# Edge keys broadcast by DMA in place of 51 transpositions on TensorE

## The reference

```python
mask = jnp.full((N, N), -jnp.inf, dtype=dtype)
mask = mask.at[src, dst].set(w[edge_type - 1])      # 6528 edges, N = 384
```

## Time and profile before

| | us |
|---|---|
| median of 3 runs | 727.94 |
| lowest and highest | 725.6, 729.39 |
| profiled execution | 726.86 |
| its span | 725.1 |
| TensorE matmuls busy | 702.6 |
| VectorE busy | 476.5 |
| ScalarE busy | 402.0 |
| Pool busy | 229.2 |

### The profile page before, as it was taken

The page is one execution under the profiler, slowest core; times in us unless marked ns, Lnnn a source line. Parts: engine busy times, 40 slices in busy tenths (PEclk is TensorE's granted clock), DMA queues, the critical chain, the costliest instruction groups (busy, mean ns, idle before and its releaser), DMA issues.

```text
span 725.1 us, 11736 instructions
## 1 busy us (share of the span) xinstructions
PE 702.6 (97%) x4490; PEld 669.4 (92%) x4490; DVE 476.5 (66%) x957; ACT 402.0 (55%) x692; POOL 229.2 (32%) x203
## 2 busy tenths in 40 slices
PE   3999999999999999999999999999999998999987
PEld 3989999998999999999999999998899998889886
DVE  6758774874777477766666565656766466787543
ACT  5455556464565565768686775422523457677340
POOL 4634332232332332227022274470004511422120
PEclk9999999999999999999999999999999999999998
DMA  5421635413313223231313152234135749896242
GB/s 212 160 107 59 231 138 211 176 60 120 109 67 117 73 102 117 90 118 58 117 59 117 59 209 73 109 121 138 41 136 193 272 164 378 307 413 220 117 145 88
DMA packets 21766, 105.15 MB, mean 145 GB/s; under 512 B 5696, under 2 KB 6080, under 8 KB 12912
## 3 DMA queue, kind: packets, MB, share of 16 engines
q1 hardware_dynamic: 12880, 80.84, 30.4%
q0 software_dynamic: 8544, 23.41, 8.9%
q10 hardware_dynamic: 288, 0.14, 0.1%
HBM read 92.71 MB, written 18.06 MB: 153 GB/s over the span
## 4 chain that ended last, share of the span: by engine, by line
PE 87%; DVE 6%; ACT 3%; DMA 2%; issue 1%; DVEq 0%; ACTq 0%
PE g_bank L1772 37%; PE g_bank L1797 12%; PE o_bank L1847 4%; PE t_bank L1836 4%; PE s_bank L2150 2%; PE s_bank L1824 2%; PE s_bank L1825 2%; PE g_bank L1726 2%; PE s_bank L2398 2%; PE s_bank L2360 2%; PE s_bank L2358 2%; PE s_bank L2359 2%; PE t_bank L2150 2%; DVE w_lo L1138 1%; PE g_bank L2332 1%; PE t_bank L2251 1%
## 5 line engine op out<-in xcount | busy, mean ns | idle before, releaser
L1772 PE MATMUL g_bank<-act_hi,w_hi 128*128 128x384 f32 x488 | 170.0, 348 | 0.0
L1772 PE MATMUL g_bank<-act_hi,w_lo 128*128 128x384 f32 x488 | 163.7, 335 | 0.0
L1772 PE MATMUL g_bank<-act_lo,w_hi 128*128 128x384 f32 x488 | 163.4, 335 | 0.0
L1138 DVE TENSOR_TENSOR w_lo<-raw,w_hi 128x2048 fp32r<-128x2048 f32 x58 | 137.3, 2367 | 36.0 <-ACT w_hi L675 34.0
L675 ACT ACTIVATE w_hi<-raw 128x2048 fp32r<-128x2048 f32 x67 | 128.1, 1912 | 30.3 <-PE s_bank L2150 12.5
L490 POOL DMA_INDIRECT edge_table<-ew,eidx x51 | 68.2, 1336 | 164.3 <-DMA edge_table<-ew,eidx 158.0
L1772 PEld LDWEIGHTS g_bank<-act_hi,w_hi 128*128 128x128 f32 x488 | 91.8, 188 | 2.7 <-issue 2.6
L1772 PEld LDWEIGHTS g_bank<-act_lo,w_hi 128*128 128x128 f32 x488 | 91.9, 188 | 0.0
L1772 PEld LDWEIGHTS g_bank<-act_hi,w_lo 128*128 128x128 f32 x488 | 91.6, 188 | 0.0
L437 POOL TENSOR_TENSOR w_lo<-raw,w_hi 128x2048 fp32r<-128x2048 f32 x10 | 47.0, 4695 | 103.5 <-ACT w_hi L675 97.2
L1275 DVE TENSOR_TENSOR pT_lo<-t_bank,pT_hi 128x384 fp32r<-128x384 f32 x96 | 50.6, 554 | 33.6 <-ACT pT_hi L768 33.2
(11 more groups left out here) (324 smaller groups left out, 1643.5 us busy)
## 6 DMA issues: line engine op xcount, KB each, us to landing
raw<-wstream_dram SPq DMA_DIRECT2D x68, 1024.0 KB, 4.8
xg<-xs POOLq DMA_DIRECT2D x12, 512.0 KB, 7.9
ys<-y_ring POOLq DMA_DIRECT2D x12, 512.0 KB, 4.6
x_sb<-x_dram SPq DMA_DIRECT2D x3, 512.0 KB, 5.0
y_acc<-x_dram POOLq DMA_DIRECT2D x3, 512.0 KB, 5.7
out_dram<-out_sb SPq DMA_DIRECT2D x6, 256.0 KB, 2.0
edge_table<-ew,eidx POOLq DMA_INDIRECT x51, 2.5
edge_table<-mask POOLq DMA_DIRECT2D x1, 576.0 KB, 3.5
```

The source lines that it names most:

```text
L1138: V.tensor_tensor(flat(w_lo[to][:, :, :]), raws[raw_slot(n.base)], flat(w_hi[to][:, :, :]), ALU.subtract) \
L1772: last = mm(out, w2[a], x2[b], start=k == 0 and a + b == 0, stop=not after and k == KT - 1 and a == 1)
```

## The change

The keys no longer go through TensorE. The host passes src and dst a second time, laid out as 51 consecutive edges in each partition (`erows`). SP loads them behind the first two weight units. Pool casts them and makes src * 384 + dst. SP writes the keys to memory as one list (`krow`), and then loads the list into all 128 partitions in two DMAs: `key_a` (the 24 columns of tiles 0 to 5, 12 KB in each partition) and `key_b` (27 columns). VectorE's comparisons read `key_a` and `key_b` in SBUF where they read `s_bank` in PSUM; tile 0 waits for the first DMA and tile 6 for the second. TensorE's 51 transpositions go, and the first head's scores no longer wait for the last comparison.

```diff
         @block.sync
             for s in range(2):
                 sp.dma_start(raw[:, s, :], wstream[s]).then_inc(raw_in[s], 16)
+            sp.dma_start(erow_i[:, :, :], erows).then_inc(erow_in, 16)
+            sp.wait_ge(erow_ready, 1)
+            sp.dma_start(krow.rearrange("(p e) -> p e", p=P), erow[:, 0, :]).then_inc(krow_out, 16)
+            sp.wait_ge(krow_out, 16)
+            split = 4 * KEY_SPLIT * P
+            sp.dma_start(key_a[:, :], krow[0:split].partition_broadcast(P)).then_inc(key_in[0], 16)
+            sp.dma_start(key_b[:, :], krow[split:E].partition_broadcast(P)).then_inc(key_in[1], 16)
             for n in range(2, UNITS):
...
         @block.gpsimd
             own.done(nc.gpsimd.memset(mask0[:, :, :], -BIG))
+            pool.wait_ge(erow_in, 16)
+            own.done(nc.gpsimd.tensor_copy(erow[:, :, :], erow_i[:, :, :]))
+            own.done(nc.gpsimd.tensor_scalar(erow[:, 0, :], erow[:, 0, :], float(N), None, ALU.mult))
+            nc.gpsimd.tensor_tensor(erow[:, 0, :], erow[:, 0, :], erow[:, 1, :], ALU.add).then_inc(erow_ready, 1)
             pool.wait_ge(raw_in[0], 16)
...
             def key_tile(c):
-                dve.wait_ge(key_full, c + 1)
+                if c % KEY_SPLIT == 0 and c // KEY_SPLIT < 2:
+                    dve.wait_ge(key_in[c // KEY_SPLIT], 16)
                 if c:
                     dve.wait_ge(key_free, c)
                 for j in range(min(4, ET - 4 * c)):
                     e = 4 * c + j
-                    last = V.scalar_tensor_tensor(junk[:, j, :], s_bank[c % 3][:, j * P:(j + 1) * P], ekey[:, e:e + 1],
+                    keys, at = (key_a, e * P) if c < KEY_SPLIT else (key_b, (e - 4 * KEY_SPLIT) * P)
+                    last = V.scalar_tensor_tensor(junk[:, j, :], keys[:, at:at + P], ekey[:, e:e + 1],
                                                   tri[:, :], ALU.is_equal, ALU.mult, accum_out=edup[:, e:e + 1])
                 last.then_inc(key_free, 1)
...
         @block.tensor
-            def key_tiles(c):
-                if c == 0:
-                    pe.wait_ge(key_ready, 1)
-                if c >= 3:
-                    pe.wait_ge(key_free, c - 2)
-                for j in range(min(4, ET - 4 * c)):
-                    e = 4 * c + j
-                    last = nc.tensor.transpose(s_bank[c % 3][:, j * P:(j + 1) * P],
-                                               ekey[:, e:e + 1].to_broadcast([P, P]), ident[:, :])
-                last.then_inc(key_full, 1)
...
             def in_V(t, k):
-                if (t, k) in ((0, 1), (0, 5), (1, 1)):
-                    key_tiles(10 + ((0, 1), (0, 5), (1, 1)).index((t, k)))
                 if (t, k) == (1, 6):
-                    pe.wait_ge(key_free, KEY_TILES)
                     head_scores("mix", first, 0)
```

More of the change, by code:

```diff
@@ L226, with program @@
 KEY_TILES = (ET + 3) // 4
+KEY_SPLIT = KEY_TILES // 2
 PR = 6
 TTR_START = 3.0e38
-def program(nc, x, wstream, ecols, pp_in, table, w1m, w2m, bo, bout, nodes, leaf_b, xs, xsel, ys, out):
+def program(nc, x, wstream, ecols, erows, pp_in, table, w1m, w2m, bo, bout, nodes, leaf_b, krow, xs, xsel, ys, out):
     with ExitStack() as ctx:
@@ L256, in program @@
         to_x, to_q, to_k, to_v = (slots01 + pad + i * tile8 for i in range(4))
-        (w4_hi,), (_, act_hi), (_, w1_raw, w1_hi, w1_lo, row_e), (_, mask01), (_, mask0, diag), \
+        (w4_hi,), (_, act_hi), (_, w1_raw, w1_hi, w1_lo, row_e), (_, mask01), (_, mask0, diag, erow_i, erow), (_, key_a), \
             (_, oTm_hi, oTg_hi, y_acc, node_raw, node_hi, node_lo, neg_leaf, nsel, h_tmp, dec, lev1, lev2, lev3, sel,
@@ L266, in program @@
                 [("hi_to_pad2", [P, slots01], F32), ("mask01", [P, 2, N], F32)],
-                [("hi_to_v", [P, to_v], F32), ("mask0", [P, NT, N], F32), ("diag", [P, 2, P], F32)],
+                [("hi_to_v", [P, to_v], F32), ("mask0", [P, NT, N], F32), ("diag", [P, 2, P], F32),
+                 ("erow_i", [P, 2, ET], I32), ("erow", [P, 2, ET], F32)],
+                [("hi_to_k3", [P, to_k], F32), ("key_a", [P, 4 * KEY_SPLIT * P], F32)],
                 [("hi_to_x2", [P, to_x], F32), ("oTm_hi", act3, F32R), ("oTg_hi", act3, F32R), ("y_acc", [P, NT, D], F32),
@@ L282, in program @@
         (w4_lo,), (_, act_lo), (_, hid, w2bd, eidx, ew), (_, mask2, rinv), \
-            (_, ecol_i, ecol, ekey, edup, etmp, tri, junk), (_, oTm_lo, oTg_lo, bo_b, bout_b), (_, h_lo), (_, raw3, xg3), \
+            (_, key_b), (_, ecol_i, ecol, ekey, edup, etmp, tri, junk), (_, oTm_lo, oTg_lo, bo_b, bout_b), (_, h_lo), (_, raw3, xg3), \
             (vf_lo, _, pTf_lo, _, qf_lo, kf_lo, xg01, selT, sel_g) = region(
@@ L290, in program @@
                 [("lo_to_pad2", [P, slots01], F32), ("mask2", [P, N], F32), ("rinv", [P, NT, 2, DH], F32)],
+                [("lo_to_k3", [P, to_k], F32), ("key_b", [P, E - 4 * KEY_SPLIT * P], F32)],
                 [("lo_to_v_half", [P, to_v + tile8 // 2], F32), ("ecol_i", [P, 3, ET], I32), ("ecol", [P, 3, ET], F32),
@@ L363, in program @@
         o_free = sem("o_free")
-        key_ready, key_full, key_free = sem("key_ready"), sem("key_full"), sem("key_free")
+        key_ready, key_free = sem("key_ready"), sem("key_free")
+        erow_in, erow_ready, krow_out = sem("erow_in"), sem("erow_ready"), sem("krow_out")
+        key_in = [sem(f"key_in{s}") for s in range(2)]
         soft_a, soft_v = sem("soft_a"), sem("soft_v")
@@ L1902, in _ @@
             first = Index(0)
-            def in_K(m, k):
-                if (m, k) in ((0, 4), (1, 0), (1, 4)):
-                    key_tiles(((0, 4), (1, 0), (1, 4)).index((m, k)))
             def in_A(m, k):
-                if (m, k) in ((0, 2), (0, 7), (1, 4)):
-                    key_tiles(3 + ((0, 2), (0, 7), (1, 4)).index((m, k)))
                 if (m, k) == (0, 4):
@@ L1921, in in_Q @@
             def in_Q(m, k):
-                if (m, k) in ((0, 0), (0, 4), (1, 0), (1, 5)):
-                    key_tiles(6 + ((0, 0), (0, 4), (1, 0), (1, 5)).index((m, k)))
                 if (m, k) == (1, 2):
@@ L1927, in in_V @@
             def in_V(t, k):
-                if (t, k) in ((0, 1), (0, 5), (1, 1)):
-                    key_tiles(10 + ((0, 1), (0, 5), (1, 1)).index((t, k)))
                 if (t, k) == (1, 6):
-                    pe.wait_ge(key_free, KEY_TILES)
                     head_scores("mix", first, 0)
-            gemm_T(Index(U_K0), act_hi, act_lo, T_X, between=in_K, hi_first=True)
+            gemm_T(Index(U_K0), act_hi, act_lo, T_X, hi_first=True)
             gemm_T(Index(U_A0), act_hi, act_lo, T_X, between=in_A)
@@ L2516 @@
         "ecols": ecols,
+        "erows": np.stack([arr(n).reshape(P, ET) for n in ("src", "dst")], axis=1),
         "pp_in": pp,
@@ L2532 @@
         args[name] = [nc.dram_tensor(f"{name}{f}", shape, F32).ap() for f in range(2)]
+    args["krow"] = nc.dram_tensor("edge_keys", (E,), F32).ap()
     args["out"] = nc.dram_tensor("out_dram", (N, D), F32, kind="ExternalOutput").ap()
```

## The result

The changed kernel took 731.87 us in the median of 19 runs (728.97 to 733.78). The kernel before, on the same chip, took 728.22 us in 19 runs (725.38 to 729.39). The medians are 3.65 us apart, and the ratio is 1.0048, with a 95% interval of 1.0033 to 1.0063. The prediction had no change, and a range up to 731.5.

What follows compares the result with a forecast made beforehand. TensorE, busy 97% of the span, was taken as the bound. Of 5.6 us saved, waits of 0.9, 1.4 and a last one left 0.4, taken as 0 against the risk: 727.9 us median, range 722.4 to 731.5.

Steps and rivals of the forecast that it cites:

- The exclusion between two SBUF inputs and Pool: First 65 us: a VectorE comparison with two SBUF inputs waits out Pool's w_lo, 4.6 us long, three times.
- The first rival, full saving: Short comparisons slip in beside Pool, no tile is late, 5.1 us gained, 722.8 us; chance 0.19.
- The head: Start: edge rows land at 13.1, Pool's cast ends at 16.25, TensorE wants it at 16.98; costs nothing.
- Steps 1 to 3: Unit 0's w_lo later, free; tile 0 at 27.0, TensorE waits 0.9 for K's take; tiles 2 to 5 cost nothing.
- The broadcasts: SP's two key loads to all partitions land at 22.8 and 27.0, unit 2 behind them at 29.5, hidden.
- the second rival: Broadcasts at half rate, 210 GB/s, delay unit 2: 6.3 us wait at TensorE, 3.9 us slower, 731.9; chance 0.15.
- that rival's sign of 33: ScalarE's w_hi of unit 2 coming past 33 us would show that the slow queue was right.
- Step 4: Pool's w_lo of unit 3 holds tile 7; Q's take ends at 50.5, TensorE waits 1.4 for the bank.
- Step 5: Tile 9 ends at 52.8, before Pool's w_lo of unit 4 at 53.1; tiles 10 to 12 end at 60.8.
- Step 6: Before the first head's transpositions: TensorE waits for normalisations until 64.6, against 64.96 before; 0.4 us gained.
- order of arrivals at 53 us: Whether tile 9 beats Pool's w_lo of unit 4; if it loses, TensorE is 1.0 us worse than before.

Runs made afterwards that it cites:

- Experiments 1: The changed kernel with the triangle copied to a PSUM bank and read there by the comparisons, first scores waiting for the last comparison; 725.83 us, ratio 0.9971.
- experiment 5: The kernel before, transpositions kept, with the comparisons reading a same-shaped SBUF tile instead of the transposed keys in PSUM; 733.95 us, ratio 1.0078.
- experiment 6: The changed kernel with the triangle in PSUM, edge rows loaded on ScalarE's queue and keys written by Pool's own DMA; 723.49 us, ratio 0.9942.
- experiment 8: The changed kernel, triangle in SBUF, with edge rows on ScalarE's queue, keys written by Pool, and comparison tiles 10 to 12 moved later; 735.55 us, ratio 1.0128.
- Experiment 4: The changed kernel with 22 matmuls that nothing reads put into TensorE's wait before the first head transposition; 729.08 us, ratio 1.0028.
- Experiment 2: The changed kernel without the edge rows' load, Pool's preparation, the key write and both broadcasts, keys held constant; 729.84 us, ratio 1.0026.
- experiment 3: The changed kernel with all 51 transpositions back on TensorE, their result read by nothing; 733.75 us, ratio 1.0078.
- experiment 7: The changed kernel, triangle in SBUF, with tile 10 behind the normalisations and tiles 11 and 12 behind heads 0 and 1; 739.78 us, ratio 1.0174.
- experiment 9: The changed kernel with tile 10 behind the normalisations and tiles 11 and 12 ahead of the w_lo behind head 0's work; 726.69 us, ratio 0.9997.

## Why the prediction was wrong

The prediction had the exclusion right and its sum wrong: the measured median is some 4 us above the forecast 727.9. Step by step:

- **The exclusion between two SBUF inputs and Pool: right, in kind, size and place.** It forecast a comparison held to the end of each of Pool's w_lo, at about 21 to 26, 44, and 53 to 57 us. They ended at 26.3, 49.5 and 59.0. The 0.34 us of nearly all others, and the one comparison by which Pool cuts in, are as forecast. Experiments 1 and 5 show that it is the cause. The first rival, full saving, fell here.
- **The head: wrong.** "I put the edge rows at 13.1 ... the step costs nothing" is the first step that failed. The rows were issued at 3.48 and were there 11.6 us later, at 15.1, though they are 51 KB. Pool's three operations took 1.3 us (15.17 to 16.47; assumed 1.2), and the cast ended at 18.31 instead of 16.25. TensorE waited 1.06, and its last norm transposition came 0.3 late. That 0.3 is not the change's: the transposition starts as late (15.40 against 15.02) in experiment 5, which has no new transfer. The K unit's product ended at 25.17, where before it was 23.67 with a tile of 0.35 in it: 1.85 us lost by then, 0.4 of it by the pace of the matmuls that experiment 6 is about. Experiment 6 removes the wait.
- **Steps 1 to 3.** Pool's late cast held VectorE's making of `ekey` (16.71 to 18.38), and w_lo of unit 0 ended at 21.8 (21.3), free as forecast. Tile 0 ended at 27.2 (forecast 27.0), the take of K at 28.3 (28.1). TensorE did not wait 0.9 for it, since it was late itself; with the head in time and the triangle in SBUF it does (experiment 8). The hidden layer's wait was 0.2. So the head's 1.85, less the 0.9 not waited here, plus 0.2, makes TensorE some 1.2 us later than forecast from here on.
- **The broadcasts: right, but unit 2 behind them came later than forecast.** They were issued 1.6 us late and landed at 25.2 and 29.5 (forecast 22.8 and 27.0), at 335 to 400 GB/s. Unit 2, issued at 21.80, took 10.8 us and landed at 32.6 (29.5), later than the 31.4 from which the second rival counted a wait. ScalarE's split began at 32.72, just short of that rival's sign of 33, and of its 6.3 us of wait came the 0.2 for the hidden layer, since TensorE was itself late.
- **Step 4.** TensorE waited 1.0 for the take of Q (1.4).
- **Step 5: right that tile 9 gets through** (it ended at 53.8; Pool began at 54.27), 1.0 to 1.2 us later than forecast, like everything behind the head. The tiles ended at 62.0 (60.8).
- **Step 6: wrong in what TensorE waits for.** It named the normalisations as what TensorE would wait for, and let the six matmuls of the next unit go before them, hidden in the wait. Those six need the bank that the take of V frees, and the take stands behind the maxima. TensorE stood 3.9 us before them and then still had them to do. About 0.5 us of the sum below falls to this.
- **The clock was no term of the sum.** In the chain the six matmuls took 2.26 us at half clock (65.08 to 67.34). Experiment 4, at full clock, needs 0.9 us less for them, so some 1.0 us in this execution is the clock.

From the forecast 64.6 to the measured 67.34 in the chain are 2.7 us: 1.2 from the head by way of step 5, 0.5 from the order in step 6, and 1.0 of clock. Against before that is 2.4 us of the 3.65. The rest is in no profile; it goes with the lower mean clock of half of the runs, and what lowers it there is not shown. The prediction said that its order of arrivals at 53 us decided the sign. That order held, and the 0.4 us that it left as a gain was less than the 1.2 of the head alone. The range was a little too narrow for the same reason: above 730.5 it had only the slow queue, with no case for a late load or for the clock.

The Trainium skill (SBUF — State Buffer, Who interferes with whom) says that a VectorE instruction with two SBUF inputs contends with a Pool instruction that reads SBUF. These traces agree: each comparison that was due while Pool's w_lo ran lasted to its end, up to 4.7 us for one of 0.34, and none was spared for being short.

## What to carry to other kernels

Before an operand moves from PSUM to SBUF, look at what the same engine's other input is: two SBUF inputs on VectorE make even a 0.34 us instruction wait for a 4.6 us one of Pool, and the cure may be to put the small constant operand into PSUM. When work is taken off the busiest engine, list for each of its next steps all that the step needs (bank, weights, and what stands ahead of the engine that frees the bank), not only the step that ended last before. And when work is moved later to make room, follow its result to its farthest reader: the comparisons had 15.6 us to spare, seen only behind a chain of 231, and that chain differed by some 17 us from one profile to another.

## What the runs showed of the hardware

- **A small load beside large ones is late by far more than its size.** 51 KB, issued at 3.48 us behind 2 MB on SP's queue, took 11.6 us to land. In experiment 6 the same load, issued at 1.73 on ScalarE's queue, still took 8.2 us. So 1.8 of the 5.2 us gained are the earlier issue and 3.4 the other queue or the earlier time; these two are not separated.
- **TensorE's clock after a wait.** In the change the granted clock fell to 0.50, that is 1.2 GHz, at about 64.5, while TensorE still stood, and stayed there for some 2.8 us after the restart at 65.08. Experiment 2, with a wait of the same 3.9, had 0.50 for 5.4 us after it, and experiment 3, with 3.2, for 5.8. In experiment 7, with a wait of 8.5 us at 314 to 322, it was 0.50 in the 5 us from 320. So a stall can cost more than its length, by an amount that differs from kernel to kernel; experiment 4, in which 22 matmuls that nobody reads fill the stall, kept 1.00 and was faster than the change by 2.7 us. The windows of experiment 7 (us, PE, PEld, DVE, ACT, POOL, clock, DMA):

```profile
315.00:320.00 5.00, 0.00 (x0) 0.00 (x0) 0.00 (x0) 0.00 (x0) 3.39 (x5) 0.87 0.21 59
320.00:325.00 5.00, 2.52 (x9) 2.42 (x10) 3.14 (x7) 2.52 (x7) 4.50 (x4) 0.50 0.17 59
```

- **The exclusion works both ways.** In experiment 9 Pool's operation on 51 columns, 0.43 us otherwise, took 2.40 beside VectorE's w_lo of 2.29 (69.42 to 71.71). POOL's group for it:

```profile
L502 POOL TENSOR_SCALAR edup<-edup x1: 2398/2398/2398, 69.6 to 69.6; 128x51 f32<-128x51 f32 x1
```

What stays open: why the half-clock stretch differs in length from one profile to another, and what sets the pace of unit 0's product at a granted clock of 1.00. It is also open what gives the change its two groups of runs: the kernel before has two as well (in the first batch about 725.5 us at a mean clock of 0.999 or 1.000, and about 728.3 at 0.995), so the stall need not be all of it.
